# Edge convolution of a graph network: spherical harmonics in the edge products instead of in the one-hot matrices

## The reference, cut to what matters

```
h0 = x0 @ W_lin1_0 * z / 8                       h1[:, :, c] = x1[:, :, c] @ W_lin1_1 * z / 8
hid = silu(edge_attr_8 @ fc_w0 / sqrt(8));       wA, wB, wC, wD = split(hid @ fc_w1 / 8)
sh0 = edge_attr_4[:, 0];                         sh1 = edge_attr_4[:, 1:4]
midA = wA * h0[src] * sh0                        midD = wD * sum_c(h1[src][c] * sh1[c]) / sqrt(3)
midB[c] = wB * h0[src] * sh1[c]                  midC[c] = wC * h1[src][c] * sh0
y = segment_sum over dst of (midA, midD, midB, midC), then two small matmuls, scaling and a residual
```

## Time and profile before

| what | value |
|---|---|
| median of 3 runs | 3518.95 us (3518.66 to 3522.92) |
| profiled execution: its span, the only time on record for it | 4581.9 us |
| front stage, in the profile | 107 us |
| convolution, first to last gather | 1699.7 us, 104 steps, clock 0.74 |
| first and second attention layer, the same | 1309.4 and 1307.0 us, clock 0.53 and 0.50 |
| busy over the span: PE, DVE, ACT, POOL | 3134.4, 2415.9, 1756.2, 2565.8 us |

### The profile page before, as it was taken

The page is one execution under the profiler, slowest core; times in us unless marked ns, Lnnn a source line. Parts: engine busy times, 40 slices in busy tenths (PEclk is TensorE's granted clock), DMA queues, the critical chain, the costliest instruction groups (busy, mean ns, idle before and its releaser), DMA issues. The chain is left out here.

```text
span 4581.9 us, 78327 instructions
## 1 busy us (share of the span) xinstructions
PE 3134.4 (68%) x20204; PEld 1904.6 (42%) x20205; DVE 2415.9 (53%) x7011; ACT 1756.2 (38%) x6334; POOL 2565.8 (56%) x2634
## 2 busy tenths in 40 slices
PE   7677777667677777477767776776466667666666
PEld 5344444344444444244444444444244334433433
DVE  6444554444455445355555555555355555555555
ACT  6122211121222122355555554554345445554554
POOL 6554444444444443566666666663566666666663
PEclk8777777777777777555555555555555555555555
DMA  7222222222222222333333333332333333333332
GB/s 238 84 86 83 81 81 81 78 80 85 82 80 82 82 85 74 99 102 103 102 105 101 103 102 106 100 102 76 99 101 101 106 105 100 101 109 100 102 101 81
DMA packets 241741, 442.78 MB, mean 97 GB/s; under 512 B 83665, under 2 KB 134933, under 8 KB 241567
## 3 DMA queue, kind: packets, MB, share of 16 engines
q0 software_dynamic: 119808, 334.13, 26.7%
q1 hardware_dynamic: 121887, 108.14, 7.7%
HBM read 381.95 MB, written 60.10 MB: 96 GB/s over the span
## 5 line engine op out<-in xcount | busy, mean ns | idle before, releaser
L1673 POOL DMA_INDIRECT nodes<-z_rows,scratch x1664 | 1674.4, 1006 | 1048.6 <-issue 501.9
L1111 POOL DMA_INDIRECT scratch<-h_rows,scratch x832 | 817.1, 982 | 892.7 <-DVE nodes L1261 676.2
L1635 ACT ACTIVATE nodes<-nodes 128x64 f32<-128x64 f32 x3328 | 816.3, 333 | 6.2 <-issue 6.2
L1155 PE MATMUL ce_part<-nodes,scratch 128*32 128x128 f32 (+1 forms) x6656 | 459.4, 391 | 151.0 <-issue 133.9
L1748 PE MATMUL ge_part<-nodes,scratch 128*32 128x260 f32 x3328 | 449.9, 633 | 5.7 <-ACT nodes L1635 5.7
L1640 ACT COPY scratch<-ge_part 128x260 f32<-128x260 f32 x208 | 78.1, 375 | 958.2 <-issue 635.0
L1909 DVE TENSOR_TENSOR_SCAN scratch<-scratch,ge_runs 1x36 f32<-1x36 f32 x208 | 45.1, 217 | 755.3 <-remote 685.7
L1723 PE MATMUL ge_runs<-ident,scratch 1*36 1x1 f32 x832 | 76.4, 192 | 527.9 <-DVE scratch L1910 491.9
L1289 DVE TENSOR_TENSOR nodes<-nodes,ce_sum 128x512 f32 x105 | 72.3, 689 | 660.7 <-remote 389.9
L1155 PEld LDWEIGHTS ce_part<-nodes,scratch 128*32 128x32 f32 x6656 | 254.9, 139 | 360.3 <-issue 299.0
L1135 PE MATMUL ce_w<-fc_sb,scratch 64*128 64x256 f32 x1664 | 313.1, 507 | 107.6 <-ACT scratch L1030 95.4
(11 more groups left out here) (271 smaller groups left out, 5538.3 us busy)
## 6 DMA issues: line engine op xcount, KB each, us to landing
nodes<-z_rows,scratch POOLq DMA_INDIRECT x1664
nodes<-hT SPq DMA_DIRECT2D x56, 256.0 KB
scratch<-h_rows,scratch POOLq DMA_INDIRECT x832
z_rows<-scratch SPq DMA_DIRECT2D x28, 264.0 KB
z_rows<-nodes SPq DMA_DIRECT2D x28, 264.0 KB
hT<-scratch SPq DMA_DIRECT2D x28, 256.0 KB
hT<-nodes SPq DMA_DIRECT2D x28, 256.0 KB
nodes<-x_rows SPq DMA_DIRECT2D x28, 256.0 KB
```

The costliest lines, as they stand in the source:

```text
L1111: nc.gpsimd.indirect_dma_start(xg[u][:, i * D:(i + 1) * D], None, m.h_rows, bass.IndirectOffsetOnAxis(ap=idx[r][:, k:k + 1], axis=0)).then ...
L1155: ins = nc.tensor.matmul(here, hots[u][:, at:at + TW], these, start=(q == 0 and c == 0), stop=(q == 1), skip_group_check=True)
L1635: ins = nc.scalar.activation(head_rows(r, k, h), head_rows(r, k, h), ACT.Copy, scale=zg[r][:, at:at + 1])
L1673: nc.gpsimd.indirect_dma_start(zg[r][:, k * ZW:(k + 1) * ZW], None, m.z_rows[layer], bass.IndirectOffsetOnAxis(ap=idx[r][:, k:k + 1], axis ...
```

## The change

The harmonics leave the one-hot matrices and go into the products. `scaled_one_hots` is gone, with its four-fold matrices; the plain one-hots of two steps are kept instead. ACT scales two of the four weight columns (wA and wC) by the first harmonic, in place in PSUM: four activations for each unit, each of 128 elements a partition. For unit 0 of step v+1 they stand right behind the silu of v+1, for unit 1 behind the copy of the tile sums. DVE forms wC' x1, then multiplies the gathered vectors in place by the three other harmonics, forms wA' x0 and wB x0, adds the three components of the scaled vectors in two operations, multiplies wB x0 by the three harmonics, and last wD by the sum of the components. A tile's block then has the eight columns of 64 that the window sum needs, and `tile_sums` has one matmul of 512 columns a tile, four a unit.

```diff
             def stage(v, r):
                 g = stage_sources(nc, act, m, v, idx[r], idx_ready)
+                nc.scalar.copy(harmonics[r], m.sh[:, bass.ds(g * (4 * G), 4 * G)])
                 stage_places(nc, act, m, v, g, staged[r], columns[r], staged_ready)
-                nc.scalar.copy(harmonics[r], m.sh[:, bass.ds(g * (4 * G), 4 * G)]).then_inc(harmonics_ready, 1)
+
+            def scale_weights(v, r, q):
+
+                act.wait_ge(w_ready, v * 2 + (q + 1))
+                if q == 0:
+                    act.wait_ge(staged_ready, v + 1)
+                for i in range(UNIT):
+                    at = (2 * i + q) * 4
+                    both = ps_w[q][:, i, 0:4:2, :]
+                    ins = nc.scalar.activation(both, both, ACT.Copy, scale=harmonics[r][:, at:at + 1])
+                ins.then_inc(w_scaled, 1)
...
                 if ahead >= 1:
                     silu(v + 1, (r + 1) % 2)
+                    scale_weights(v + 1, (r + 1) % 4, 0)
                 act.wait_ge(unit_summed, v * 2 + 4)
                 nc.scalar.copy(sums, ps_part[:, :]).then_inc(sums_ready, 1)
+                if ahead >= 1:
+                    scale_weights(v + 1, (r + 1) % 4, 1)
...
                 if q == 0:
-                    pe.wait_ge(hots_ready, v + 1)
+                    pe.wait_ge(hot_ready, v + 1)
                     pe.wait_ge(sums_ready, v + 1)
-                for c in range(4):
-                    for j in range(NB):
-                        k = 2 * j + q
...
-                        ins = nc.tensor.matmul(here, hots[u][:, at:at + TW], these,
-                                               start=(q == 0 and c == 0), stop=(q == 1), skip_group_check=True)
+                for j in range(NB):
+                    k = 2 * j + q
+                    ins = nc.tensor.matmul(ps_part[j * TW:(j + 1) * TW, :], hot[u][:, k * TW:(k + 1) * TW],
+                                           msg[q][:, j * BLOCKS * MUL:(j + 1) * BLOCKS * MUL],
+                                           start=(q == 0), stop=(q == 1), skip_group_check=True)
...
-                V.tensor_tensor(out[:, :, 0:8:7, :], w[:, :, 0:2, :], x[:, :, 0:1, :].broadcast_to([P, UNIT, 2, MUL]), ALU.mult)
-                for k in range(2):
-                    ins = V.tensor_tensor(out[:, :, 1 + 3 * k:4 + 3 * k, :], w[:, :, 2 + k:3 + k, :].broadcast_to([P, UNIT, 3, MUL]),
-                                          x[:, :, 1:4, :], ALU.mult)
-                ins.then_inc(msg_ready, 1)
...
+                V.tensor_tensor(out[:, :, 3:8:2, :], w[:, :, 2:3, :].broadcast_to(vector), vectors, ALU.mult)
+                V.tensor_tensor(vectors, vectors, turns, ALU.mult).then_inc(turned_ready, 1)
+                V.tensor_tensor(out[:, :, 1:7:5, :], w[:, :, 0:2, :], scalars.broadcast_to([P, UNIT, 2, MUL]), ALU.mult
+                                ).then_inc(by_x0_ready, 1)
+                dve.wait_ge(turned_ready, n)
+                V.tensor_tensor(x[:, :, 1, :], x[:, :, 1, :], x[:, :, 2, :], ALU.add).then_inc(pair_ready, 1)
+                dve.wait_ge(by_x0_ready, n)
+                V.tensor_tensor(out[:, :, 2:7:2, :], by_x0.broadcast_to(vector), turns, ALU.mult)
+                dve.wait_ge(pair_ready, n)
+                V.tensor_tensor(x[:, :, 1, :], x[:, :, 1, :], x[:, :, 3, :], ALU.add).then_inc(dot_ready, 1)
+                dve.wait_ge(dot_ready, n)
+                V.tensor_tensor(out[:, :, 0, :], w[:, :, 3, :], x[:, :, 1, :], ALU.mult).then_inc(msg_ready, 1)
...
                 products(v, r, 0, gathered)
                 if ahead >= 1:
-                    one_hots(v + 1, (r + 1) % 4)
+                    places(v + 1, (r + 1) % 4)
...
                 products(v, r, 1, gathered)
                 if ahead >= 1:
-                    scaled_one_hots(v + 1, (r + 1) % 4)
+                    one_hots(v + 1, (r + 1) % 4)
```

More of the change, by code:

```diff
@@ L903, in conv_stage @@
         xg = part(UNIT * D, slots=4)
-        hots = part(G * 4 * TW)
+        hot = part(G * TW)
         hidT = part(GE // 2)
@@ L946, in conv_stage @@
         got = [sem(f"gathered{u}") for u in range(4)]
[L947 to L951, removed]
+        (sp_done, idx_ready, staged_ready, pool_go, hid_ps, hid_ready, w_ready, w_scaled, by_x0_ready, turned_ready, pair_ready,
+         dot_ready, msg_ready, rel_ready, hot_ready, pick_ready, unit_summed, sums_ready, summed, added) = [
+            sem(n) for n in ("sp_done", "idx_ready", "staged_ready", "pool_go", "hid_ps", "hid_ready", "w_ready", "w_scaled",
+                             "by_x0_ready", "turned_ready", "pair_ready", "dot_ready", "msg_ready", "rel_ready", "hot_ready",
+                             "pick_ready", "unit_summed", "sums_ready", "summed", "added")]
         block = ctx.enter_context(nc.Block())
@@ L1083, in _ @@
             silu(0, 0)
+            scale_weights(0, 0, 0)
+            scale_weights(0, 0, 1)
             all_steps(act, last_quad, step)
@@ L1263, in products @@
-                ins.then_inc(msg_ready, 1)
-            def one_hots(v, r):
+                n = v * 2 + (q + 1)
+                vector = [P, UNIT, 3, MUL]
+                scalars, vectors = x[:, :, 0:1, :], x[:, :, 1:4, :]
+                turns = harmonics[r].rearrange("p (i t c o) -> p t i c o", t=2, c=4, o=1)[:, q, :, 1:4, :].broadcast_to(vector)
+                by_x0 = out[:, :, 6:7, :]
+                dve.wait_ge(unit_summed, n)
+                dve.wait_ge(w_scaled, n)
+                dve.wait_ge(got[u], gathered)
@@ L1266, in one_hots, with places @@
+                dve.wait_ge(by_x0_ready, n)
[4 more added lines that the diff above has]
+                V.tensor_tensor(out[:, :, 0, :], w[:, :, 3, :], x[:, :, 1, :], ALU.mult).then_inc(msg_ready, 1)
+            def places(v, r):
                 dve.wait_ge(staged_ready, v + 1)
@@ L1267, in one_hots @@
                 relative_places(V, rel.rearrange("p (j t) -> p j t", j=NB), staged[r]).then_inc(rel_ready, 1)
+            def one_hots(v, r):
                 dve.wait_ge(rel_ready, v + 1)
-                one_hots_of(V, m, hot, rel).then_inc(hot_ready, 1)
+                one_hots_of(V, m, hot[r % 2], rel).then_inc(hot_ready, 1)
             def node_picks(v, r):
                 picked_nodes(V, pick[r % 2], columns[r], staged[r]).then_inc(pick_ready, 1)
-            def scaled_one_hots(v, r):
-                dve.wait_ge(hot_ready, v + 1)
-                dve.wait_ge(harmonics_ready, v + 1)
-                V.tensor_tensor(hots[r % 2].rearrange("p (k c n) -> p k c n", k=G, c=4),
-                                hot.rearrange("p (k o n) -> p k o n", k=G, o=1).broadcast_to([P, G, 4, TW]),
-                                harmonics[r].rearrange("p (k c o) -> p k c o", k=G, o=1).broadcast_to([P, G, 4, TW]),
-                                ALU.mult).then_inc(hots_ready, 1)
@@ L1361, in _ @@
             V.memset(ps_sum[:], 0.0).then_inc(added, 1)
+            places(0, 0)
             one_hots(0, 0)
             node_picks(0, 0)
-            scaled_one_hots(0, 0)
             all_steps(dve, last_quad, step)
```

3 lines of the change are left out of this document (removed).

## The result

The changed kernel takes 3758.14 us (median of 4, 3756.5 to 3758.78), the kernel before 3520.84 us: a ratio of 1.068, 95% interval 1.0664 to 1.0695. It is slower by 237 us; forecast were 135, with a range up to 3745 us. The direction was right, the size was not.

A forecast was written before the change was run, and what follows sets the result against it. The prediction took POOL's gathers to bound the kernel before, at 10.3 us a step, and DVE after: 11.3 + 0.2 + 0.1 = 11.6 us. 1.3 us more over 104 steps, +135 us, gave 3654 us, range 3535 to 3745.

The forecast's parts named there:

- The floor of the gathers: POOL's back-to-back gathers bound the kernel before: 10.27 us a convolution step, 3511 us in all with the stretches without gathers.
- DVE's work: DVE's operations in a convolution step: 8.10 us before, less 1.13 and 4.68 removed, plus 8.52 added.
- DVE's own results: DVE's last product in each unit waits for the second add just before it: 0.2 us a step.
- the table read: Reading the window's base loses its cover when the one-hots move behind both units' products: 0.3 us a step.
- the chain to the next products: Tile sums, hidden layer, silu, weights and scalings between unit 0's products sometimes outlast DVE's other work: 0.2 us a step.
- beside POOL: DVE and POOL, so close in time per step, cost each other something: 0.1 us a step.
- The gathers: Convolution gathers lengthen beside DVE's two-SBUF-input operations, mean 1.05 to 1.1 us; POOL's floor 11.0 us, under DVE's.
- 1: Rival: the profile's waits are real and PE's chain bounds the runs; about -0.8 us a step, 3436 us; chance 0.08.
- 2: Rival: DVE's additions fit below POOL's floor or overlap better than the sum; unchanged at 3519 us; chance 0.07.
- 3: Rival: PE stays at 1.2 GHz, making steps longer; +2.7 us a step, 3800 us; chance 0.08.
- the DVE-bound case: DVE becomes the convolution's bound at 11.6 us a step, 3654 us; ends 10.9 to 12.4 us; chance 0.77.
- the prediction's rule: Gathers lengthen in proportion to DVE's time in operations with both inputs in SBUF; +0.12 us a gather for the change.

The follow-up runs named there:

- PE's part alone: Kernel before with one 512-column tile-sum matmul a tile, one-hots scaled by the first harmonic, other three harmonics left out; 3520.01 us, ratio 1.0001.
- second profile: The kernel before, unchanged, run and profiled once more; 3518.92 us, ratio 1.0, profile span 3521.5 us.
- PSUM input: Changed kernel, the product with the three harmonics taking its other factor from PSUM (unscaled second weight) instead of SBUF; 3758.07 us.
- the run without DVE's waits: Changed kernel without ACT's scalings, with the window's base read amid unit 0's products and the square root early on ACT; 3673.84 us.

## Why the prediction was right or wrong

- **The floor of the gathers** was right, though read from a profile whose own waits were not those of the runs: the kernel before has a step of 10.51 us for the forecast 10.3 (a gather takes 1.010 us, not 0.982), and PE's work is free (PE's part alone). The Trainium skill (Runtime: NRT & Kernel Launch, "The ~15µs preamble/postamble breakdown") has about 6 us between profile and execution. Here the measurements differ: the spans of the second profile and of the changed kernel's lie 2 us under the times of their own executions (3521.5 for 3523.48, 3755.8 for 3757.67), and the first one 1063 us over the median. A span far from the run's time marks a profile that isn't of the kernel's normal course.
- **DVE's work** was right to 1%: 8.10 - 1.13 - 4.68 + 8.52 = 10.81 us a step in the sum, 10.74 measured. Some of that is luck: before, DVE has 8.24 us for 8.10, and the change added 2.50 for 2.71. The neighbours of the trace priced operations that it didn't have (0.949 to 0.952 us for 768 elements, forecast 0.95 from the row of another shape).
- **The waits in DVE's queue** are the term that failed. The sum had 0.2 for DVE's own results, 0.3 for the table read, 0.2 for the chain to the next products and 0.1 beside POOL: 0.8 us. Measured are 1.98. The table read and the window sums take 86.3/104 = 0.83 for 0.3, and two waits of the node part had no term at all: the square root, 0.52, and the output matmuls, 0.23. The sum held only waits that the change would add, and took those that DVE had as nothing. They were 94.4 us at the window's sum and 14.3 for the output matmuls before, 86.3 and 24.3 after: the change did not make them, it took away the slack under POOL's floor that hid them. The square root's, 9.1 us before and 53.7 after, was for the most part made by the change, which put four scalings ahead of it in ACT's queue; the prediction named the staging as what is queued behind them and passed over the square root, also queued there. The two runs that take away the table read and the square root gave 45 and 46 us, and 86 together. The forecast was 102 us short, and of the waits taken away it had allowed some 31 us (0.3 x 104) for the table read.
- **The remainder**: 12.72 - 10.51 = 2.21 us a step, times 104, is 230 us of the 237 (the gap behind the convolution, 49.0 for 37.8 us, is 11 more, and the rest of the kernel a few less). The forecast had 1.3 us a step and nothing for the gap.
- **The gathers** were forecast at 1.05 to 1.1 us and have 1.094, but their floor, 11.0 us a step in the forecast and 8 x 1.396 = 11.17 measured, doesn't bind in the changed kernel (PSUM input).
- **The rivals**: 1 and 2 are out. Of 3, PE at the lower clock, only a trace is there: the clock averaged 0.79 in the convolution for 0.88 before, and PE was busy 955 us for 924 with a fifth less to do in the tile sums, and in the run without DVE's waits a chain of 1.94 + 2.08 + 2.06 us at the lower level (tile sums, weights, window sums) stands before DVE's window sum in one of the steps. What the change would cost with the clock held high wasn't tried.
- **The profile's signs** came as written: DVE near 1150 us (1117), ACT up by some 270 (566 from 348, so 218), attention unchanged (1106 and 1081 us for 1108 and 1086). The tile sums are at 285 us, not 400, because the rows that gave 499 us were of the first profile; the second has 353.
- **The range** ended at 3745. Its upper end for the DVE-bound case, 12.4 us a step, had no room for waits of the node part.

What stays open: why the steps without DVE's waits stay at 11.8 us. DVE's busy time is 10.7 us of them and the gathers' floor 8 x 1.418 = 11.3; the rest is waiting, of DVE for PE and of POOL for DVE, and no run separates the parts, nor that of the clock.

## What to carry to other kernels

Where a change makes an in-order engine the bound, go through everything in its queue in every kind of step, the rare ones too, and ask of each wait whether the old slack was all that hid it; here the waits were 1.98 of the 12.72 us, and the work alone would have stood at 10.74, next to the old bound, though no run with all of that work got under 11.8. Price what is queued behind an inserted operation on its engine, also when it runs once in four steps. And before any wait of a profile is believed, hold its span against the run's time and the sum of the plainest work, here the gathers. A wait that such a test rules out in size may still be there in kind: DVE's waits at the window's sum and for the square root were 653 and 68 us in the first profile and 94 and 9 in the second, not nothing.

## What was not expected of the hardware

- One DVE operation of 768 elements a step, 0.95 us long, cost 80 us over 104 steps with both inputs in SBUF and 18 us with one in PSUM. The gathers took 1.100 and 1.015 us. A gather that starts in the run of such operations takes 1.34 us instead of 0.95 (808.50 in the changed kernel), so the price is paid by POOL: in the changed kernel DVE's operations of 768 elements with two SBUF inputs took 0.949 and 0.952 us, none over 0.972, for the 0.952 us of the one that reads PSUM. And it is far from in proportion to DVE's time: 0.085 us a gather here, where the prediction's rule would give 0.02. The Trainium skill (SBUF — State Buffer, "Who interferes with whom") has it that a DVE instruction with two SBUF inputs contends with a GpSimd instruction that reads SBUF. These runs agree, if an indirect gather is taken for such an instruction, and give the price. The same section tells of a probe in which `tensor_tensor` did not stall DMA; for these gathers the measurement decides otherwise. Of the full block that the prediction quoted, which the section states for DVE's two-port modes, DVE's durations show nothing.
- 32 activations of 32 elements took ACT 310 ns each as busy time and 3.5 us for 16 in a row, 0.22 us apiece. The scalings, of 128 elements in PSUM, took 341 ns each and 1.11 us for four in a row, 0.28 apiece: a quarter of the elements saves a fifth of the time.
